# The tokens' stage of an alignment kernel: lengths from a squared reciprocal, mask operations on another engine

## The reference

```
D = sqrt(max(aa + bb - 2.0 * a @ b.T, 0))        # a: context rows, b: layernorm(x)
R[i, j] = D[i, j] + min(R[i-1, j], R[i, j-1], R[i-1, j-1])
path = backtrack(R);  x = x + scatter_add(small[i on path] at j on path)
x = x + ffn(layernorm(x))                        # 8-bit fixed point, 256 -> 1024 -> 256
```

## Time and profile before

| what | value |
|---|---|
| median of 3 runs | 179.82 us (179.59 to 180.24) |
| the profiled execution | 178.78 us |
| its span, first to last instruction | 177.0 us |
| busy: VectorE | 152.1 us (86%) |
| busy: PE | 115.9 us (65%) |
| busy: ScalarE | 107.8 us (61%) |
| busy: GpSimd | 40.5 us (23%) |

### The profile page before, as it was taken

How to read it: one execution, slowest core, us unless ns; L and a number is a source line. 1 busy time by engine, 2 the same in 40 slices (tenths; PEclk the granted TensorE clock), 3 DMA queues, 4 the chain that set the end, 5 groups by cost and what they waited for, 6 DMA issues and landing times.

```text
span 177.0 us, 3519 instructions
## 1 busy us (share of the span) xinstructions
PE 115.9 (65%) x1123; PEld 79.8 (45%) x1123; DVE 152.1 (86%) x732; ACT 107.8 (61%) x203; POOL 40.5 (23%) x101
## 2 busy tenths in 40 slices
PE   6999970000028698000007979999999999999991
PEld 6798960000015473000002435655666666666680
DVE  4899968999999999999999479998898999896361
ACT  3687676699998010053150089878777777878720
POOL 7964896000000000000000000014050413222250
PEclk9999996555555556755555799999999999999999
DMA  5997008400009950020203422005454637282948
GB/s 147 355 349 224 6 0 335 171 0 0 2 4 312 344 175 0 0 74 2 74 3 131 65 41 33 0 0 63 59 62 58 72 52 83 40 98 25 114 50 191
DMA packets 19554, 16.88 MB, mean 95 GB/s; under 512 B 5712, under 2 KB 19152, under 8 KB 19408
## 3 DMA queue, kind: packets, MB, share of 16 engines
q1 hardware_dynamic: 14288, 12.69, 22.5%
q0 software_dynamic: 3808, 3.67, 17.1%
q10 hardware_dynamic: 1440, 0.30, 0.8%
HBM read 7.48 MB, written 9.18 MB: 94 GB/s over the span
## 4 chain that ended last, share of the span: by engine, by line
DVE 40%; PE 38%; POOL 7%; DMA 6%; ACT 3%; issue 2%; SPq 2%; POOLq 0%; DVEq 0%; ACTq 0%
PE y L1381 14%; PE h L1362 9%; DMA X<-in_x_dram 6%; DVE R L913 6%; DVE Y L1139 5%; PE t L1362 5%; PE h L1403 3%; DVE A L885 3%; DVE carry L903 3%; DVE M L904 3%; DVE enter L1122 3%; PE e L1321 3%; POOL lengths L499 3%; DVE bcarry L1121 3%; SPq L356 2%
## 5 line engine op out<-in xcount | busy, mean ns | idle before, releaser
L520 POOL DMA_DIRECT2D out_dram<-E x14 | 17.0, 1217 | 125.7 <-DVE E L1108 125.7
L1381 PE MATMUL y<-w2T,XT 128*128 128x256 bf16 x240 | 35.8, 273 | 0.0
L1381 PEld LDWEIGHTS y<-w2T,XT 128*128 128x128 bf16 x240 | 23.3, 98 | 14.0 <-DVE XT L1052 0.3
L694 ACT ACTIVATE h_int<-h,b_s 128x512 int16<-128x512 f32 x37 | 25.3, 686 | 4.9 <-PE h L1362 4.3
L1403 PE MATMUL h<-w1T 128*128 128x512 bf16 x21 | 8.0, 546 | 23.8 <-DVE enter L1122 23.8
L1362 PE MATMUL h<-M,w1T 128*128 128x512 bf16 x74 | 21.9, 380 | 0.8 <-ACT M L687 0.7
L1301 PE MATMUL t<-ident_bf,w_raw 128*128 128x128 bf16 x32 | 4.6, 311 | 26.9 <-ACT w_raw L628 25.2
L1098 DVE TENSOR_SCALAR XT<-h_int 128x1024 bf16<-128x1024 int16 x28 | 12.1, 440 | 8.2 <-ACT h_int L694 8.2
L1301 PEld LDWEIGHTS t<-ident_bf,w_raw 128*128 128x128 bf16 x32 | 3.1, 147 | 28.4 <-issue 25.5
L1403 PEld LDWEIGHTS h<-w1T 128*128 128x128 bf16 x21 | 2.5, 130 | 28.5 <-DVE enter L1122 24.6
L694 ACT ACTIVATE h_int<-t,b_s 128x512 int16<-128x512 f32 x19 | 13.0, 686 | 3.4 <-PE t L1362 3.2
(11 more groups left out here) (239 smaller groups left out, 304.8 us busy)
## 6 DMA issues: line engine op xcount, KB each, us to landing
X<-in_x_dram SPq DMA_DIRECT2D x8, 512.0 KB, 9.0
out_dram<-E POOLq DMA_DIRECT2D x14, 256.0 KB, 4.3
w_raw<-in_L_ffn_w_dram SPq DMA_DIRECT2D x2, 1024.0 KB, 5.9
out_dram<-b_s SPq DMA_DIRECT2D x2, 1024.0 KB, 5.9
out_dram<-b_s SPq DMA_DIRECT2D x2, 768.0 KB, 9.5
S<-in_ctx_dram SPq DMA_DIRECT2D x1, 512.0 KB, 4.0
out_dram<-E SPq DMA_DIRECT2D x4, 128.0 KB, 3.2
path_dram<-A SPq DMA_DIRECT2D x3, 160.0 KB, 1.8
```

Source lines behind the costliest of these rows:

```text
L520: nc.gpsimd.dma_start(tiles_out[:, b:b + 2, quad_of(g, 2 * h), :], res[:, g % 2, 2 * h:2 * h + 2, :], accum_op=ALU.add).then_inc(out_store ...
L694: nc.scalar.activation(h_int[:, g % 2, n, :], hidden_banks[i % 3][:, :], ACT.Identity, bias=b1_s[:, n:n + 1], scale=1.0 / W_ONE).then_inc( ...
L1381: mm = nc.tensor.matmul(results(g, t, t + 1)[:, 0, :], hq[:, g % 2, n, t * P:t * P + P], w2T[:, n, :], start=(n == 0 and not bias), stop=( ...
```

## The change

Three things are changed, all in the tokens' stage.

First, the lengths. With rstd = 1 / sqrt(s / D + eps), the squared length s * rstd^2 equals D - D * eps * rstd^2. ScalarE now makes `length_gap`, the Square of rstd scaled by sqrt(D * eps), and D is put into aa as a bias. GpSimd's two operations per load subtract the gap; bb_part, bb and the copy of the sum are gone.

Second, the masks. Eight of the ten operations go to GpSimd, four behind the spread of load 0 and four behind that of load 1 (one more there, for the square that VectorE made in one operation with two steps; one fewer for Dm, whose zeros need no memset now). The two on the order numbers (`order_numbers`) stay on VectorE, behind the distances of load 1.

Third, orders and small things. VectorE takes all statistics of loads 1 to 3 without a break and now does reciprocal, transpose, product and addition of a load one after the other. GpSimd makes the lengths of load 1 ahead of the spread of load 3. GpSimd's rest of the context waits for the context's lengths. PE's lead is 11 full products of 128 columns. E is cleared only in its first 7 and last 8 slots, and two memsets move behind the lengths.

```diff
-LEAD = 40
+LEAD = 11
-            nc.gpsimd.memset(E[:, :, :], 0.0).then_inc(pool_const, 1)
+            nc.gpsimd.memset(E[:, 0:CH - 1, :], 0.0).then_inc(pool_const, 1)
+            nc.gpsimd.memset(E[:, HR:SLOTS, :], 0.0).then_inc(pool_const, 1)
             def token_lengths(k):
-                pool.wait_ge(rstd_ready, k + 1)
-                pool.wait_ge(sum_copied, k + 1)
-                nc.gpsimd.tensor_tensor(bb_part[:, k, :, :], spread_sum[:, k, :, :], rstd[:, k, :, :], ALU.mult).then_inc(length_order, 1)
-                pool.wait_ge(length_order, 2 * k + 1)
-                nc.gpsimd.tensor_tensor(bb[:, k, :, :], bb_part[:, k, :, :], rstd[:, k, :, :], ALU.mult).then_inc(length_order, 1)
-                pool.wait_ge(length_order, 2 * k + 2)
+                pool.wait_ge(gaps_made, k + 1)
...
-                        bb[:, k, e, :].rearrange("p (h c) -> p h c", h=2).unsqueeze(3).to_broadcast([P, 2, CL, HR]),
-                        ALU.add).then_inc(lengths_made, 1)
+                        length_gap[:, k, e, :].rearrange("p (h c) -> p h c", h=2).unsqueeze(3).to_broadcast([P, 2, CL, HR]),
+                        ALU.subtract).then_inc(lengths_made, 1)
             pool.wait_ge(ctx_split, 1)
+            pool.wait_ge(ctx_len_ready, 1)
             nc.gpsimd.tensor_tensor(S_r1[:, :, :], S[:, :, :], S_hi[:, :, :], ALU.subtract).then_inc(ctx_rest, 1)
-            for k in range(LOADS - 1):
-                spread_of(k)
+            spread_of(0)
+            pool.wait_ge(lane_maxima, 5)
+            nc.gpsimd.tensor_scalar(Dm[:, 1:SLOTS, 0], first[:, 0:1].to_broadcast([P, SLOTS - 1]), BIG, 0.0, ALU.mult,
+                                    ALU.add).then_inc(slot_masks, 1)
...
+            spread_of(1)
...
+            spread_of(2)
             token_lengths(0)
+            token_lengths(1)
             spread_of(LOADS - 1)
-            token_lengths(1)
             token_lengths(2)
             token_lengths(LOADS - 1)
+            nc.gpsimd.memset(b2_rows[:, :], 0.0).then_inc(pool_const, 1)
+            nc.gpsimd.memset(ones[:, :], 1.0).then_inc(pool_const, 1)
...
-                nc.scalar.activation(spread_sum[:, k, :, :], spread_bank(k), ACT.Copy).then_inc(sum_copied, 1)
+            def token_gap(k):
+                act.wait_ge(rstd_ready, k + 1)
+                nc.scalar.activation(length_gap[:, k, :, :], rstd[:, k, :, :], ACT.Square,
+                                     scale=math.sqrt(D * EPS)).then_inc(gaps_made, 1)
...
             for j in range(UL // 2):
                 copy_xT(2, j)
+                if j % 2:
+                    token_gap(j // 2)
             spread(2)
             for j in range(UL // 2):
                 copy_xT(3, j)
+                if j == 1:
+                    token_gap(2)
             roots(0)
             spread(3)
+            token_gap(3)
...
             load_moments(0)
-            for j in range(B // 2):
-                moments(1, j)
-            first_masks()
-            for j in range(B // 2, UL):
-                moments(1, j)
+            load_moments(1)
             load_moments(2)
             scales(0)
             load_moments(3)
+            scales(1)
             turned(0)
-            scales(1)
-            distances(0)
+            scaled(0)
+            lengthened(0)
+            scales(2)
             turned(1)
-            scales(2)
-            distances(1)
+            scaled(1)
+            lengthened(1)
+            order_numbers()
             turned(2)
             scales(3)
-            distances(2)
+            scaled(2)
+            lengthened(2)
...
-                nc.tensor.matmul(bank5[0:TW, 0:8], ident[:, 0:TW], ident[:, 0:8], start=True, stop=True)
+                nc.tensor.matmul(bank5[:, 0:P], ident[:, :], ident[:, :], start=True, stop=True)
```

More of the change, by code:

```diff
@@ L506, in _ @@
             nc.gpsimd.tensor_tensor(S_r1[:, :, :], S[:, :, :], S_hi[:, :, :], ALU.subtract).then_inc(ctx_rest, 1)
-            for k in range(LOADS - 1):
-                spread_of(k)
+            spread_of(0)
+            pool.wait_ge(lane_maxima, 5)
+            nc.gpsimd.tensor_scalar(Dm[:, 1:SLOTS, 0], first[:, 0:1].to_broadcast([P, SLOTS - 1]), BIG, 0.0, ALU.mult,
+                                    ALU.add).then_inc(slot_masks, 1)
+            nc.gpsimd.tensor_scalar(init0[:, :], first[:, :], -BIG, BIG, ALU.mult, ALU.add).then_inc(slot_masks, 1)
@@ new lines, in _ @@
+            nc.gpsimd.tensor_tensor(last_row[:, :], upper[:, 0:CH], lower[:, 1:CH + 1], ALU.add).then_inc(slot_masks, 1)
+            nc.gpsimd.tensor_tensor(own_slot[:, :], upper[:, :], lower[:, :], ALU.add).then_inc(slot_masks, 1)
+            spread_of(1)
+            columns = column_batch[:, :, :, :].rearrange("p e h c -> p (e h c)")
+            nc.gpsimd.tensor_tensor(other[:, :], columns, odd_batch[:, 0:1].to_broadcast([P, 2 * 2 * CH]),
+                                    ALU.subtract).then_inc(batch_masks, 1)
@@ L509, in _ @@
+            nc.gpsimd.tensor_scalar(lower_big[:, :], is_lower[:, :], BIG, 0.0, ALU.mult, ALU.add).then_inc(batch_masks, 1)
+            pool.wait_ge(batch_masks, 1)
+            nc.gpsimd.tensor_tensor(other[:, :], other[:, :], other[:, :], ALU.mult).then_inc(batch_masks, 1)
+            pool.wait_ge(batch_masks, 3)
+            nc.gpsimd.tensor_scalar(other[:, :], other[:, :], BIG, 0.0, ALU.mult, ALU.add).then_inc(batch_masks, 1)
+            spread_of(2)
             token_lengths(0)
+            token_lengths(1)
@@ L581, in _ @@
             src = bank23[0][:, :, :].rearrange("p a b -> p (a b)")[:, 0:P].rearrange("p (h i) -> p h i", h=2)
-            nc.scalar.activation(aa[:, :, 0:HR], src[:, :, 0:HR], ACT.Copy, scale=float(D)).then_inc(aa_copied, 1)
-            nc.scalar.activation(aa[:, :, HR:I], src[:, :, I - 1:HR - 1:-1], ACT.Copy, scale=float(D)).then_inc(aa_copied, 1)
+            act.wait_ge(shifts_made, len(SHIFTS))
+            at = SHIFTS.index(float(D))
+            nc.scalar.activation(aa[:, :, 0:HR], src[:, :, 0:HR], ACT.Identity, bias=shifts[:, at:at + 1],
+                                 scale=float(D)).then_inc(aa_copied, 1)
+            nc.scalar.activation(aa[:, :, HR:I], src[:, :, I - 1:HR - 1:-1], ACT.Identity, bias=shifts[:, at:at + 1],
+                                 scale=float(D)).then_inc(aa_copied, 1)
             for j in range(UL // 2):
@@ L828, in turned, with scaled @@
                                     dist_banks[k][:, :, :].rearrange("p a b -> p (a b)")).then_inc(prods_made, 1)
-            def distances(k):
+            def scaled(k):
                 v.wait_ge(prods_made, 3 * k + 1)
```

55 lines of the change are left out of this document (17 added, 38 removed).

## The result

The changed kernel takes 178.46 us in the median of six executions (177.57 to 179.37); the kernel before, on the same chip, 179.62 (179.09 to 180.24, six). The ratio is 0.9948, with a 95% interval of 0.9926 to 0.9971: 0.93 us less (0.0052 x 179.62), between 0.52 and 1.33.

A forecast was written before the change was run, and what follows sets the result against it. The prediction took GpSimd's chain of lengths, with VectorE waiting for it behind X, as the bound. 1.81 of stalls less 1.23 of holds gave 0.58: 179.82 to 179.2 us, range 177.6 to 180.4.

The forecast's parts named there:

- VectorE's walk: VectorE from the second reciprocal (19.49) to E's first transposes: 31.02 instead of 32.83 without stalls or holds, 1.81 us less.
- The holds: VectorE operations slowed beside GpSimd's writes of lengths for loads 1 to 3: three of 0.41, 1.23 us, bounds 0 and 3.57.
- the rival that leaves no gain: Holds on VectorE of 1.8 instead of 1.23, say with the order numbers held too: 179.8 us; chance 0.15.
- VectorE stands for whole writes: Rival: GpSimd wins each time, VectorE waits out whole lengths writes in three loads, price 3.57: 180.4 to 181.6 us; chance 0.12.
- Masks at 0: Moving mask operations off VectorE's statistics gains 0, bounds 0 and 0.15, as VectorE then waits for X.
- X at 18.0: Load of X: its last piece, issued at 7.8, lands at 18.0 as before and sets the end of the statistics.
- stood at nothing in the sum: PE's shorter lead: counted as no gain or loss, being ahead of 19.49 on an engine outside the chain, covered by X.
- The rival on X: A later instruction fetch lets X land one piece earlier, 1.4 us more won: 177.8 us; a fetch at 13 delays it; chance 0.13.
- Its sign: Sign that the forecast is right: VectorE's last four statistics still start near 18.1, with a wait for X ahead.
- ScalarE with nearly 1 us to spare: ScalarE's queue in the tokens' stage: first half's roots done by 30.5, VectorE's last half near 31.4; cost 0.
- a wait in this queue: ScalarE's added Squares: each stands for VectorE's reciprocal with later work queued behind it; cost 0.
- What 32.83 gains is what the kernel gains: From E's first transposes (32.83) on: hardly anything is edited, so the stage's gain was taken as the whole kernel's.

The follow-up runs named there:

- a_nolengths: The changed kernel without the writes of lengths of loads 1 to 3, the first load's lengths added instead; 177.53 us, ratio 0.9886 to the kernel before.
- a_masks: The changed kernel with the eight mask operations back on VectorE, amid the second load's statistics; 178.21 us, ratio 0.9937 to the kernel before.
- a_repeat: The changed kernel itself, unchanged, run once more in ten executions; 178.81 us, ratio 0.9977 to the kernel before.
- a_mid: The changed kernel with the order numbers back in the middle of the second load's statistics on VectorE; 177.22 us, ratio 0.9896 to the kernel before.
- a_mid_turned: As a_mid, with the first two loads' transposes ahead of the next loads' reciprocals on VectorE, as before the change; 177.93 us, ratio 0.9926.
- a_lead40: The changed kernel with PE's lead of before, 40 small products in place of 11 full ones; 178.58 us, ratio 0.9968 to the kernel before.

## Why the prediction came out as it did

It said 179.2 us, 0.6 less than before; the kernel gained 0.93 (0.52 to 1.33) in one set of executions and 0.41 (0.0023 x 179.27, in relative terms less than the 0.3% that the prediction took for what can be told) in the other. The sign was right, and so was the mechanism of the sum: waits for lengths go and smaller holds come. One term of it is no constant, and the forecast lies between the two gains partly by luck: X has two places and not one, and the holds fell in part on other operations than it had them.

**VectorE's walk.** 1.81 us once no wait for lengths is left: right. The sum from the second reciprocal to E without holds was 31.02 - 19.49 = 11.53; `a_nolengths`, which has none, measured 11.61.

**The holds.** 1.23 forecast, as three of 0.41; 1.33 measured. The size was right and the parts were not: the additions of loads 0 and 2 at 0.30 each, none on load 1's (the write that started beside it at 23.00 held the order numbers behind it), and 0.42 and 0.30 on the order numbers. These I had free of holds in the sum and held only in the rival that leaves no gain. The Trainium skill (VectorE: DVE Perf Modes, the perf-mode tier table), which that rival named for tensor_scalar in fp32, agrees with the trace here: the order numbers, both tensor_scalar with one input (of int32, for which that table has no column), are held beside GpSimd (0.67 against 0.25). That rival was half right, in its mechanism and not in its total: beside the order numbers it had all of the 1.23, and what was held there was two additions at 0.30. The transposes, as I had it, and the statistics were not held.

**VectorE stands for whole writes**, the slower rival, did not happen in this place: an addition lost 0.30 beside a pair of writes of 1.19. Something like it happened to order_low beside memsets, 2.48 us, in one profile. The Trainium skill (SBUF — State Buffer, Who interferes with whom) says that between GpSimd and a VectorE instruction in a two-port mode whoever issues first has the shared ports for its whole instruction while the other blocks. The trace agrees that VectorE blocks, but not for how long: the longest of those memsets was 0.54, and order_low lasted through all of them.

**Masks at 0.** Right, as the times of `a_masks` (0.9937 against 0.9948 and 0.9977) show. The reason given, that X's last piece sets the end of the statistics, holds in `a_repeat` (a wait of 1.37) and in `a_masks` (0.76). With X early it is weaker, by the estimated 0.5 above.

**X at 18.0.** This is the term that was mis-sized, and with it the lead, which stood at nothing in the sum though it moves the fetch: the piece lands at 16.9 to 17.3 in half of the profiled executions with a short lead and at 18.0 to 18.55 in the other half. The rival on X had both halves of it, the later fetch and that a fetch then hits the last piece, and gave 0.13 to what half of the profiles show, at 0.7 to 1.1 us before 18.0 and not 1.4. Its sign, that the last four statistics still start near 18.1, failed in the profile of after (17.23) and held in `a_repeat` (18.21). In `a_repeat`, where X is late, the steps stand nearly where they were put: the second reciprocal at 19.53 (19.49), E's transposes at 32.47 (32.25).

**ScalarE with nearly 1 us to spare**, right for this order: the last roots waited 0.89 us for VectorE. It was not much: once VectorE's walk was shorter, the fourth load's deviation was late by 0.22 (`a_mid`) and 0.96 (`a_mid_turned`), by the Square that the prediction had as a wait in this queue and priced at 0.

**What 32.83 gains is what the kernel gains**: only within some tenths. From E's transposes to the end of the span it is 144.2 before (177.0 - 32.83), 144.3 after, 144.4 in `a_repeat`, and 145.0 in `a_lead40` (177.3 - 32.26), with no edit there. So the span of a single profile is no measure of 0.3 us even where its first part is understood to 0.1.

## What to carry to other kernels

Ask first whether the profiled execution is typical: where a kernel's times scatter by 1.8 us and its profile is the shortest of them, a wait that is missing there may be a chance of that execution, and one more profile of the same program says so. Price a moved operation by what runs beside it at its new place, GpSimd's memsets included: the same two small operations cost 0.51 us among statistics, 1.23 beside writes of lengths and 2.74 beside memsets. And change one part at a time before a bundle is kept: here one edit gave 1.5 us and the bundle around it gave part of that back, until the order numbers and GpSimd's order were put back where they had been. Where an engine stands for an input that comes late, look at what set that input's start: here it was a wait in the queue of its producer, several operations ahead of it.

## What the runs showed of the hardware

- Where a fetch of 16 KB of instructions fell at 10.3 to 10.5 us, beside the fifth piece of a load, the last of that piece's sixteen landings came 1.1 to 1.5 us behind the fifteenth in four of four executions, and 0.75 to 1.5 us in the pieces behind it. Where it fell at 15.8 to 16.4, pieces five to seven were whole in ten of ten, and the last piece was late in five. That one DMA engine is held by the fetch is my reading; no row names the engine. On the page of after that queue has 0.3% of the sixteen engines' span, so nothing in a view of totals points to it.
- VectorE's order_low took 2.48 us, in one profile, beside a run of GpSimd memsets of 0.1 to 0.54 us each, while the additions beside pairs of writes lost 0.30.
- GpSimd is held as well: a pair of writes of 1.19 us took 1.64 to 1.90 beside VectorE's products and additions.
